# The 48 transfers of turned maxima issued from ScalarE's queue in place of SyncE's

## What is computed

```python
xn = layernorm(x)
x = x + attn0(xn) + block(xn)      # attn0: 16 heads of 8, causal
                                   # block: ln, causal attention, ln, top 2 of 8 experts (128 to 512 to 128), all computed densely
xn = layernorm(x)
x = x + attn1(xn) + moe(xn)        # attn1: 16 heads of 8, not causal
                                   # moe: top 2 of 8 experts; two groups of four 128-wide ones
```

## Time and profile before

| | |
|---|---|
| Median of 3 runs | 775.28 us (771.7 to 775.81) |
| Profiled execution, its time | 773.3 us |
| Its span, first to last instruction | 771.6 us |
| PE busy | 735.7 us (95%), granted clock 0.986 |
| DVE busy | 586.9 us (76%) |
| ACT busy | 499.5 us (65%), 623 instructions |
| POOL busy | 184.5 us (24%) |
| DMA queue of SP / of ACT | 13.9% / 0.5% of the 16 DMA engines' span |

### The profile page before, as it was taken

How to read it: one execution, slowest core, us unless ns; L and a number is a source line. 1 busy time by engine, 2 the same in 40 slices (tenths; PEclk the granted TensorE clock), 3 DMA queues, 4 the chain that set the end, 5 groups by cost and what they waited for, 6 DMA issues and landing times.

```text
span 771.6 us, 16158 instructions
## 1 busy us (share of the span) xinstructions
PE 735.7 (95%) x6366; PEld 401.4 (52%) x6366; DVE 586.9 (76%) x1162; ACT 499.5 (65%) x623; POOL 184.5 (24%) x425
## 2 busy tenths in 40 slices
PE   5789999999999999999999999999999999999998
PEld 2433545776435465556544446566544566743344
DVE  5999995376999786468898887664888643589984
ACT  6177664547787656655778764746687683377784
POOL 5255451022441003013541100020652000010000
PEclk8699999999999999999999999999999999999999
DMA  5334530000302000030310110030030000021000
GB/s 156 85 95 142 174 94 3 17 3 5 89 6 55 24 16 3 25 85 3 82 31 3 51 43 3 4 91 4 17 95 5 1 1 3 1 64 31 17 5 14
DMA packets 34907, 31.70 MB, mean 41 GB/s; under 512 B 10280, under 2 KB 33200, under 8 KB 34608
## 3 DMA queue, kind: packets, MB, share of 16 engines
q1 hardware_dynamic: 33488, 29.09, 13.9%
q10 hardware_dynamic: 1152, 1.05, 0.5%
q0 software_dynamic: 192, 0.52, 0.3%
HBM read 7.32 MB, written 1.05 MB: 11 GB/s over the span
## 4 chain that ended last, share of the span: by engine, by line
PE 75%; DVE 11%; ACT 11%; issue 2%; POOL 1%; DMA 0%; ACTq 0%; DVEq 0%; POOLq 0%
PE psum L969 18%; PE psum L891 14%; PE psum L956 14%; PE psum L870 8%; PE psum L843 8%; DVE neg_max L507 6%; ACT probs L768 4%; PE psum L820 3%; ACT probs L744 3%; ACT L768 2%; ACT L744 2%; PE psum L823 2%; PE psum L918 1%; PE psum L848 1%; PE psum L903 1%
## 5 line engine op out<-in xcount | busy, mean ns | idle before, releaser
L507 DVE TENSOR_REDUCE neg_max<-psum 128x2 f32<-128x1024 f32 (+2 forms) x320 | 345.1, 1112 | 79.1 <-PE psum L848 52.0
L744 ACT ACTIVATE probs<-psum 128x1024 f32<-128x1024 f32 (+1 forms) x320 | 288.4, 938 | 113.8 <-PE psum L870 112.5
L891 PE MATMUL psum<-probs,v_ones 128*25 128x512 f32 (+3 forms) x1536 | 151.6, 492 | 0.1
L768 ACT ACTIVATE probs<-psum,col 128x512 f32<-128x512 f32 x160 | 98.7, 688 | 52.9 <-PE psum L956 52.5
L969 PE MATMUL psum<-ew,probs 128*128 128x128 f32 x1024 | 128.6, 279 | 0.0
L969 PEld LDWEIGHTS psum<-ew,probs 128*128 128x128 f32 x1024 | 120.3, 192 | 15.8 <-issue 13.5
L843 PE MATMUL psum<-k_stack,q_stack 64*128 64x512 bf16 (+3 forms) x768 | 115.3, 332 | 11.4 <-ACT probs L744 4.3
L956 PE MATMUL psum<-normed_T_a,ew 128*128 128x512 f32 x256 | 117.3, 597 | 0.0
L1054 POOL TENSOR_SCALAR_AFFINE_SELECT probs<-probs 128x512 f32<-128x512 f32 x128 | 81.2, 643 | 139.7 <-ACT probs L744 138.1
L870 PE MATMUL psum<-q_stack,k_stack 64*128 64x512 bf16 (+3 forms) x768 | 107.8, 327 | 6.4 <-ACT probs L744 3.3
L668 DVE SCALAR_TENSOR_TENSOR acc<-psum,gate,acc 128x128 f32<-128x128 f32 x256 | 72.0, 344 | 36.5 <-PE psum L969 32.5
(11 more groups left out here) (131 smaller groups left out, 580.4 us busy)
## 6 DMA issues: line engine op xcount, KB each, us to landing
q_stack<-part SPq DMA_DIRECT2D x66, 128.0 KB, 2.4
k_stack<-part SPq DMA_DIRECT2D x66, 128.0 KB, 2.5
ew<-w_expert_in SPq DMA_DIRECT2D x4, 512.0 KB, 4.6
ew<-w_expert_out SPq DMA_DIRECT2D x4, 512.0 KB, 5.2
q_stack<-k_stack SPq DMA_DIRECT2D x14, 128.0 KB, 2.3
q_stack<-maxT SPq DMA_DIRECT2D x48, 32.0 KB, 1.9
x_in<-x SPq DMA_DIRECT2D x4, 256.0 KB, 3.0
out<-acc SPq DMA_DIRECT2D x4, 256.0 KB, 2.6
```

The costliest lines, as they stand in the source:

```text
L507: eng.tensor_reduce(neg_max[:, q % 2, :, xs[0]:xs[-1] + 1, i], src, AX_X, ALU.max, negate=True).then_inc(vector_done.sem, 1)
L744: eng.activation(dst, src, ACT.Exp, scale=SCALE).then_inc(probs_ready.sem, 1)
L768: ins = eng.activation(probs[:, order.slot[step[:-1]], 2 * k + f, :], two_banks(step)[:, f, :], ACT.Gelu_apprx_tanh if layer else ACT.Gelu ...
L891: ins = eng.matmul(sum_bank[32 * c:32 * c + V_COLS, q0:TILES * P], v_ones[u][:, j, g // 2 * QH + c, col0:col0 + V_COLS], probs[:, order.sl ...
```

## The change

The branch of the step "max_turn" moves from SP's walk over the order to ACT's. The wait, the transfer, its semaphore and the step's place in `SCORE` stay. Lines behind line 754 shift by 8, so the issue is line 760 now.

```diff
@@ -752,6 +752,14 @@
                     eng.activation(head_sums[:, q % 2, :], sum_bank,
                                    ACT.Copy).then_inc(scalar_done.sem, 1)
                     assert scalar_done.count() == order.act[step]
+                elif kind == "max_turn":
+                    u, g = step[2:]
+                    q = order.max_quads.index((b, u, g))
+                    slot, x0 = order.stacks[b, u], 2 * g
+                    eng.wait_ge(vector_done.sem, order.dve[step])
+                    eng.dma_start(q_stack[slot][MAX_BLOCK:P:BLOCKS, x0:x0 + 2, :],
+                                  maxT[:, q % 2, :]).then_inc(max_landed[q % 2].sem, 16)
+                    max_landed[q % 2].count()
                 elif kind == "gate_exp":
@@ -1114,14 +1122,6 @@
                         fill_piece(eng, step, 0)
                         fill_piece(eng, step, 1)
-                elif kind == "max_turn":
-                    u, g = step[2:]
-                    q = order.max_quads.index((b, u, g))
-                    slot, x0 = order.stacks[b, u], 2 * g
-                    eng.wait_ge(vector_done.sem, order.dve[step])
-                    eng.dma_start(q_stack[slot][MAX_BLOCK:P:BLOCKS, x0:x0 + 2, :],
-                                  maxT[:, q % 2, :]).then_inc(max_landed[q % 2].sem, 16)
-                    max_landed[q % 2].count()
                 elif kind == "store":
```

## The result

The changed kernel takes 793.42 us in the median of 4 runs (792.99 to 793.72), the kernel before 775.54 beside it (4 runs, 771.7 to 775.94). The ratio is 1.024, with an interval from 1.0218 to 1.0263. That is 18 us slower, where the prediction had 8 and ended its range at 792. The profiled execution took 793.72 us around a span of 792.0, 20.4 us more than the span before.

The account below looks back on a forecast made before the run. The prediction took PE, busy 735.7 of 771.6 us, as the bound, so that delays making PE wait count. Early transfers 3.0 plus the rest 5.1 gave 8.1 us, hence 783.3 us against a 775.28 median, range 776 to 792.

Parts of the forecast that it names:

- the serial count of 25.8 us: Total delay on ACT over 48 transfers if each issue starts only after the ACTIVATE before it ended; 20.5 us otherwise.
- The half of the rule that rows 5 could not confirm: On ACT, the sequencer pushes an ACTIVATE and goes on, so a DMA issue runs beside it; ACT's profiled issues left this open.
- each against the next ACTIVATE of the order: On ACT, each copy's end plus 0.60 us compared with the next ACTIVATE's start; sum over 48 copies 20.5 us.
- the share of 0.3 for the rest: Of the remaining 17.1 us of ACT delay, 0.3 was to reach PE: 5.1 us, with bounds of 0 and 0.6.
- the upper end: Slowest forecast, 792 us: 25.8 x 0.6 = 15.5 us, plus 1.4 us for the loads, on 775.3.
- 3.0 us for the early two: At the second and third transfers, ACT's exponents come 1.69 us later each; 3.0 of 3.4 us reach PE.
- The loads of weights going out early: On SP, loads follow straight behind x and compete with transfers of the first 60 us: nothing counted, at most 1.4 us.
- a late last transfer: If its issue waits for ACT's exponents, it comes 1.1 us late, 0.3 us more than there is room.
- much over 1.9: Sign against the prediction: transfers issued from ACT taking much longer to land than the 1.9 us median.
- (a): Rival: ACT's idle time hides the delay, leaving half of 3.0 us, 776.8 us, no measurable change; chance 0.17.
- (b): Rival: faster, as transfers no longer stand behind stack fills in SP; 4.1 us come back, 771.2 us; chance 0.04.
- (c): Rival: ACT's issues are slower than SP's on shared DMA engines; six jams add 10 us, 793 us; chance 0.09.

Follow-up runs that it names:

- experiment 2: Kernel before, with ScalarE also issuing an unread transfer of zeros at each place, without waiting for the copy: 774.43 us, ratio 0.9998.
- Experiment 6: Changed kernel with the 13th and 36th transfers back on SyncE, the other 46 on ScalarE: 789.26 us, ratio 1.0192.
- experiment 9: Changed kernel with only the first four transfers back on SyncE, the other 44 on ScalarE: 790.65 us, ratio 1.0205.
- experiment 1: Kernel before, SyncE still issuing, with ScalarE only waiting for the copy at each place: 777.06 us, ratio 1.004.
- Experiment 7: Kernel before with only the first four transfers moved to ScalarE, the other 44 on SyncE: 780.14 us, ratio 1.0077.
- experiments 1 to 4: First four follow-up kernels; the third, the changed kernel with each issue one ScalarE step later, took 782.04 us. Kernel before beside the four: median 775.08 us.
- experiment 4: Changed kernel, but SyncE still waits for each copy at the old place, so weight loads go out as before: 792.31 us, ratio 1.0246.
- experiment 5: Kernel before, real transfers on SyncE, with ScalarE waiting for each copy and then issuing an unread transfer: 792.25 us, ratio 1.0231.
- experiment 11: Kernel before with 19 transfers on ScalarE, where its next instruction started at least 0.62 us behind the copy's end: 774.76 us, ratio 1.0008.

## Why the prediction was wrong in size

**Right: the mechanism.** 47 of the 48 issues stand on ACTq 0.03 us behind their copies (the 27th 0.48 us, behind the issue of the 26th). An instruction of ACT behind a transfer starts no sooner than 0.62 us behind the copy's end in the trace after (0.60 was reckoned). PE gets its exponents late, is late from 41 us on, and never catches up.

**Right: the issue runs beside the earlier ACTIVATE.** Around the fourth transfer of the changed kernel (ACT's timeline):

```profile
62.35 1.02 ACT L744 ACTIVATE probs<-psum 128x1024 f32<-128x1024 f32 x1 [0.16 <-PE psum L878]
62.85 0.54 ACTq L760 DMA_DIRECT2D q_stack<-maxT  x1
63.44 0.60 ACT L752 ACTIVATE head_sums<-psum 128x512 f32<-128x512 f32 x1
```

The issue starts 0.52 us before the ACTIVATE ahead of it has ended. So the serial count of 25.8 us was not needed. The half of the rule that rows 5 could not confirm (the Trainium skill, Perfetto Trace Analysis, DVE / Act Engine Instruction: the sequencer is free for the next instruction once it has pushed an ACTIVATE) agrees with this trace and with experiment 2.

**Wrong, the first step: "each against the next ACTIVATE of the order".** The instruction to compare with was ACT's next one, a table load where there is one. With it, and with 0.62 us, the sum over the same rows of before is 23.9 us and not 20.5: the 13th transfer holds ACT up by 1.74 us (166.88 + 0.62 - 165.76), the 36th by 1.45. Against the next ACTIVATE they were 0.42 and 0.14 us in the prediction's count. Experiment 6 prices this at 3 to 4 us. The changed trace shows the 36th too (PE's timeline):

```profile
557.13 0.39 PE L878 MATMUL psum<-q_stack,k_stack 64*128 64x512 bf16 x2 [1.69 <-ACT probs L744]
```

**Wrong, the second step and the largest: the share of 0.3 for the rest.** This is the term of 5.1 us. The transfers from the fifth on hold ACT up by 18.7 us by the corrected count, and PE's lag grows by 13.7 behind 60 us, of which 1.3 are the landing of the seventh. That is 12.4 of 18.7, a share of 0.66, where I took 0.3 of 17.1 and let the upper end stop at 0.6. Without the two table loads (1.8 and 1.5 us of lag for 3.2 us of delay) it is 9.1 of 15.5, or 0.59: the prediction's upper bound was about the true value. In medians, the term of 5.1 us measured 17.9 - 6.2 = 11.7 (16.4 by experiment 9). A part of it, at transfer 44, goes with the 3.4 us at half clock. I had taken the half of the places where PE is not waiting to pass nothing. But 29 of the 48 delays are above nought, and they are not alike. If each place absorbs its first 0.3 us, and passes the rest in full, the later ones pass 11.8 us of the 18.7. For the wait alone, without table loads and without the issue, the same rule gives 2.0 us, and experiment 1 shows 1.4 behind the early part. That fits both and is no more than a fit (with the 0.03 us that experiment 1's trace shows, the 2.0 become 1.8), but it would explain why the wait alone and the issue alone cost so little: at 0.06 us behind the copy 10 of the 48 delays are over 0.3 us, at 0.62 us behind it 24, and at the first 10 of these all of the added 0.56 us passes. A single share does not fit both kernels (1.4 of 5.0 us for the wait alone is 0.28, against 0.66); a threshold for each place does.

**Too small: 3.0 us for the early two.** Experiment 7 measured 6.2. All of the first four hold ACT up by 5.1 us (1.31, 1.72, 1.72, 0.35); I named 3.4 for two and left the first in the rest. The fourth copy, forecast some 3 us late, ends 6.6 us late (62.82 against 56.25). The remainder may be the clock, which the prediction did not have at all. In the profiled execution before it is at half for 3.4 us from 33.4 on, in the one after for 17.1 us from 31.7 and again for 3.4 from 55.6. The first of these began before the first transfer was issued (32.1), and a kernel as fast as the one before (experiment 2) has 13.7 us at half clock between 30 and 50 us, so most of it cannot be laid to the change. What that costs can be estimated from runs of the kernel before itself. Of those beside experiments 1 to 4, the ones with a mean clock of 0.992 took 771.6 to 771.9 us, the ones with 0.98 775.9 to 776.3, so 0.012 of clock goes with about 4.4 us. The changed kernel's four runs have 0.976 to 0.982, the middle of those before is 0.987. That makes some 2 to 4 us of the 18 by that estimate. No run here holds the clock while it delays PE, so the split stays an estimate.

**Bounds that held.** The loads of weights going out early cost nothing that the total shows (experiment 4); the last transfer was not late. Nor was it the tightest: before, the 38th had 0.71 us between its landing and its scores, the last 0.84, and the seventh 1.24. (The 0.3 us for a late last transfer, meant for the upper end, are missing from its sum of 16.9.) The seventh was late: ACT's timeline, and PE's:

```profile
86.47 0.54 ACTq L760 DMA_DIRECT2D q_stack<-maxT  x1
...
93.23 0.39 PE L878 MATMUL psum<-q_stack,k_stack 64*128 64x512 bf16 x2 [1.32 <-DMA q_stack<-maxT]
```

Its landing took 6.7 us, and SP had issued four weight loads between 84.5 and 87.8 us. The prediction had named a landing "much over 1.9" as a sign against it. It is worth 1.3 us, and in experiment 5, with the real transfer on SyncE, there is no such step in PE's lag, yet the total is the same.

**The rivals.** (a) ACT's idle time hides it: not for the 48, but fully for the 19 of experiment 11. The Trainium skill's sentence that the sequencer's time to start a DMA is usually small beside the DMA (DMA: Bandwidth & Descriptors, Issuing engines are not separate DMA queues) agrees with the issue alone, 0 us in experiment 2. The 18 us of experiment 5 come with the wait ahead of the issue, which the prediction charged. (b) Faster through SyncE's queue: no run came out measurably faster. (c) ACT's issues jam: the slowest of 48 took 0.612 us, so that its figure of 793 is nearly the measured 793.4 is luck: the cause is another.

## What to carry to other kernels

Before a DMA with a wait is moved to a computing engine's queue, take for each transfer the end of what it waits for plus the issue (here 0.62 us), and compare it with the start of the next instruction of that engine, table loads included. Where it was later, PE, busy for 95% of the span, lost nearly all that exceeded some 0.3 us (a fit on this kernel alone); where it was earlier, the move was free (19 transfers). Do not price the wait and the issue apart and add them, for here 2 us and 0 us made 18.

## What the runs showed of the hardware that I had not expected

- A wait written ahead of an exponent became part of the exponent's ACTIVATE, and its table load went ahead of it (start at 541.75, copy's end at 542.55). A DMA issue that waits held the table load too (176.69, behind the issue at 176.05).
- A stretch of 3.4 us at half clock begins between 54.6 and 57.0 us, about where PE's wait behind the third transfer ends, in all five traces in which ScalarE waits and issues there, and in none of the other eight; at half clock pairs of matmuls took 0.61 us in place of 0.39. The stretches between 30 and 50 us come to 3.4, 13.7 and 10.2 us in the traces of three kernels of the same time (before, experiments 2 and 11), and to 17.1 in the changed one. In experiment 2, whose median is that of before, the trace has 6.8 us of it from 40.5 on, and PE lies 1.7 to 2.0 us behind from there to the end. That may be much of the spread from 771.6 to 776.3 us of the kernel before.
- A transfer of 32 KB took 6.7 us to land beside four weight loads where the median is 1.9. With two weight loads behind it the same transfer took 5.1 and 5.4 us in experiments 4 and 5, and 3.3 before.
